# A two-layer decoder on one core: the causal masks of the self-attentions are written into the PSUM banks ahead of the scores, in the scores' own tile shape

## The chip, the cores and the metric

The kernel runs on one core of a Trainium2 chip. The metric is the device time of one execution in microseconds, as the median of several runs. A profile of one further execution gives the trace from which rows are quoted; it has its own time.

## The reference

Eight sequences of 128 tokens with 512 features pass through two post-norm decoder layers. Layer 0 is causal self-attention with 32 heads of 16 features, a cross-attention by autocorrelation against a context, and a mixture of low-rank experts. Layer 1 is causal self-attention with normalised queries and keys and a slope per head (ALiBi), a cross-attention with grouped keys, and a low-rank feed-forward. The change touches the two self-attentions alone:

```python
scores = jnp.einsum('bhqd,bhkd->bhqk', q, k) / math.sqrt(hd)       # layer 0
causal = jnp.tril(jnp.ones((l, l), bool))
scores = jnp.where(causal, scores, -jnp.inf)
att = jax.nn.softmax(scores, axis=-1)
...
scores = jnp.einsum('bqhd,bkhd->bhqk', q, k) * scale               # layer 1
scores = scores + slopes[None, :, None, None] * rel[None, None]
scores = jnp.where(causal[None, None], scores, jnp.float32(-1e+30))
probs = jax.nn.softmax(scores, axis=-1)
```

## The kernel before

A self-attention walks over eight sequences in four steps each (`STEPS = 4`), 32 steps in all, and a step covers eight heads. Queries and keys lie transposed in `qk`, two heads to a strip of 32 partitions (`PAD = 32`): 16 rows of features and beside them rows that carry the slope, the position, block masks (a query block may not see a later key block) and, once known, the row's maximum. So one matmul with 32 rows of contraction gives one head's 128 x 128 scores.

Every step issues two sets of such matmuls from `scores(l, i)`. The first set (L997, step i) writes scores with queries on partitions into the two banks `s_bank`; VectorE takes the maxima of their rows (`maxima`, L2342). The second set (L1002, step i - 5, since `LAG = 5`) writes scores with keys on partitions, with the maxima already subtracted, into the two banks `t_bank`; ScalarE exponentiates them (L1584), and `weigh_values` (L1017) multiplies with the values. Each set has eight matmuls of 32 x 128 weights and 128 columns; four to a bank, and a bank belongs to one strip of 32 rows of the array. The two sets of a step use opposite strips, so that four strips work side by side. Float32 matmuls stand in the trace as two records each.

Only the four diagonal 32 x 32 blocks of each head still need a causal mask. `hide_later` adds it after the scores: per bank four bf16 matmuls of an identity block (32 x 32 weights, `ident16`) with the mask's block repeated for four heads (`causal16`, 32 x 128), each to 32 partitions. The 16 matmuls of a full step fall on the 16 different 32 x 32 tiles of the array. The last of them signals `scores_psum` or `shifted_psum`, for which VectorE and ScalarE wait.

Between two calls of `scores`, TensorE has other work that is written out in a fixed order per step: projections of coming sequences (`mm3`, L840 to L842, three matmuls for a product of split float32r operands), transposes (L949, L890), the output projection, and in a sequence's first step the transpose of its predecessor's maxima (L959). In a sequence's first step the scores also wait for rows that DMAs write into `qk`: in layer 0 and 1 eight `extra` rows (L758 on the SyncE queue, L1565 on ScalarE's for two sequences), signalled by `extra_loaded`, and the maxima (L749), signalled by `max_loaded`. All engines run in the order in which their instructions are written; semaphores tie them together.

Of the kernel before, what the change touches and what calls it, by code (L numbers as in the profile page):

```python
# [13 lines left out]
P = 128  # L14
# [13 lines left out]
RING = 3  # L28
# [19 lines left out]
def shape_constants():  # L48

    t = np.arange(L)  # L50
    ck, sk = np.arange(L // 2 + 1), np.arange(1, L // 2)

    cos_e = lambda n, f: np.cos(2 * np.pi * np.outer(n, f) / L)
    sin_e = lambda n, f: np.sin(2 * np.pi * np.outer(n, f) / L)
    same = np.concatenate([cos_e(t, ck), sin_e(t, sk)], 1)
    swap = np.concatenate([sin_e(t, ck), cos_e(t, sk)], 1)
    weight = np.where((ck == 0) | (ck == L // 2), 1.0, 2.0)

    inv1 = np.concatenate([weight * cos_e(t, ck), 2 * cos_e(t, sk)], 1).T / L
    inv2 = np.concatenate([-weight * sin_e(t, ck), 2 * sin_e(t, sk)], 1).T / L  # L60

    ctx_even = same.copy()
    ctx_even[L - 1, 0] += L

    odd = np.arange(1, 2 * L, 2)[: L // 2]
    ang = lambda n: 2 * np.pi * np.outer(n, odd) / (2 * L)
    lag_odd = np.concatenate([np.cos(ang(t)), np.sin(ang(t))], 1)
    full = np.arange(2 * L)
    co, so = np.cos(ang(full)), np.sin(ang(full))  # L70
    hold = lambda m: np.concatenate([m[: L - 1], m[L - 1:].sum(0, keepdims=True)], 0)
    ctx_odd = np.concatenate([hold(co), hold(so)], 1)
    ctx_odd_swap = np.concatenate([hold(so), hold(co)], 1)

    oute1 = np.concatenate([weight * cos_e(t, ck), 2 * cos_e(t, sk)], 1).T / (2 * L)
    oute2 = np.concatenate([weight * sin_e(t, ck), -2 * sin_e(t, sk)], 1).T / (2 * L)
    outo1 = np.concatenate([2 * np.cos(ang(t)), 2 * np.cos(ang(t))], 1).T / (2 * L)
    outo2 = np.concatenate([2 * np.sin(ang(t)), -2 * np.sin(ang(t))], 1).T / (2 * L)
    tables = [same, ctx_even, swap, ctx_odd, ctx_odd_swap, lag_odd, inv1, inv2, oute1, oute2, outo1, outo2]
    dft = np.stack(tables, 1).astype(np.float32)  # L80

    slopes = (1.0 / np.power(2.0, np.arange(1, H + 1, dtype=np.float32) * (8.0 / H))).astype(np.float32)
    later = np.where(t[:PAD][None, :] > t[:, None] % PAD, -1e30, 0.0)
    sooner = np.where(t[:, None] % PAD > t[:PAD][None, :], -1e30, 0.0)
    masks = np.concatenate([np.eye(P), later, sooner], 1)
    row = np.arange(P) % PAD
    scale, shift = np.zeros((P, 4)), np.zeros((P, 4))
    for which in range(2):
        own, aug = row // HD == which, HD * (1 - which)
        scale[own, which], scale[own, 2 + which] = HD ** -0.5, 1.0  # L90
        shift[row == aug, 2 + which] = 1.0
    extra = np.zeros((2, 2, GROUPS, 4, 2, KT, P))
    head = HT * np.arange(KT)[None, None, :] + 2 * np.arange(GROUPS)[None, :, None] + np.arange(2)[:, None, None]
    extra[1, :, :, 0, 0] = slopes[head][..., None]
    extra[:, :, :, 0, 1] = t - L / 2.0
    for j in range(GROUPS - 1):
        extra[:, :, :, 1 + j, 0] = t // PAD == j
        extra[:, :, :, 1 + j, 1] = np.where(t // PAD > j, -1e30, 0.0)
    small = np.concatenate([scale, shift], 1)
    first_rows = np.repeat(shift[:, :, None], L, 2)  # L100
    for e in range(2):
        for g in range(GROUPS):
            at = g * PAD + HD * (1 - e) + 1
            first_rows[at:at + 4, e:e + 3:2] = extra[0, e, g, :, :, 0]
    return {
        "dft": dft, "masks": masks.astype(np.float32), "small": np.ascontiguousarray(small.astype(np.float32)),
        "extra": extra.astype(np.float32), "first_rows": first_rows.reshape(P, 4 * L).astype(np.float32),
    }
# [7 lines left out]
def decoder(nc, a, out):  # L116
# [9 lines left out]
    with es:  # L126
        place = [ARENA]

        def sb(name, shape, dt=F32):

            at = place[0]
            place[0] += -(-(2 if dt == BF16 else 4) * int(np.prod(shape[1:])) // 32) * 32
            assert place[0] <= ARENA_END, (name, place[0])
            return nc.alloc_sbuf_tensor_at(name, shape, dt, offset=at)
# [55 lines left out]
        (DX, DC, DCS, DO, DOS, DL, I1, I2, E1, E2, O1, O2) = [table[:, i * P:(i + 1) * P] for i in range(12)]  # L190
        br_row = sb("br_row", [P, LH])
        ident = sb("ident", [P, P])
        ident16, causal16 = sb("ident16", [P, P], BF16), sb("causal16", [P, 2, PAD], BF16)
        small = sb("small_sb", [P, 8 + 6 * KT])
        qk_scale, qk_shift = [sb(f"qk_{n}", [P, 2, 2, KT]) for n in ("scale", "shift")]
        row_scale, row_shift = small[:, 0:4], small[:, 4:8]
# [38 lines left out]
        def view(s, at, n, parts=P):  # L235
            return tank[s][0:parts, at:at + n]
# [5 lines left out]
        tok = [view(1, 768 + 512 * i, 512) for i in range(2)]  # L242
        staged = [view(1, 768 + 2 * D * i, 2 * D) for i in range(2)]
        bv_row, bo_row = [view(1, 2816 + D * i, D) for i in range(2)]
        causal = view(1, 3840, 2 * PAD)

        def values_of(s, e):

# [184 lines left out]
        xo_ready = per_slot("xo_ready")  # L433

        TABLES, EARLY, ROWS = 2, 3, 3
        CLOCKED = 17
        W0_TILES = 2 * KT
        X_AT, O_AT = ((0, 1), (1, 1), (1, 0)), (0, 0)
# [162 lines left out]
        def shared(i):  # L602

            return i // STEPS, i % STEPS % 2, i % STEPS // 2
# [12 lines left out]
        def tiles(ap, k=KT):  # L617
            return ap.rearrange("p (k t) -> p k t", k=k)
# [216 lines left out]
        def _(pe):  # L835
# [122 lines left out]
                bank_taken(u)  # L958
                nc.tensor.transpose(m_bank[u % 2][:, 0:P], nm[b % 2], ident[:, :]).then_inc(m_full[u % 2], 1)  # L959

            def hide_later(banks, turned_over):

                for n in range(2):
                    for g in range(GROUPS):
                        rows = (g + 2 * turned_over + n) % GROUPS
                        at, of = slice(g * PAD, (g + 1) * PAD), slice(rows * PAD, (rows + 1) * PAD)
                        ins = mm(tiles(banks[n][:, :])[at, :, at], ident16[of, of],  # L967
                                 causal16[of, turned_over, :].unsqueeze(1).broadcast_to([PAD, KT, PAD]), start=False, stop=True,
                                 skip_group_check=True)
                return ins  # L970

            def scores(l, i):

                j = i - LAG
                if scored(i):
                    b, rows, e = shared(i)
                    if i % STEPS == 0:
                        if (l, b) == (0, 0):
                            pe.wait_ge(first_k, 1)
                            pe.wait_ge(tables_ready, TABLES)  # L980
                        else:
                            pe.wait_ge(qk_rows, batch(l, b, 2, 2))
                            pe.wait_ge(extra_loaded[b % 2], 16 * 2 * GROUPS * (l * B // 2 + b // 2 + b % 2))
                    if l == 0 and i == 2:
                        pe.wait_ge(qk_rows, batch(0, 0, 2, 2))
                    pe.wait_ge(max_ready, step(l, i - 1, 2))
                if scored(j):
                    c, rows_c, f = shared(j)
                    if j % STEPS == 0:
                        pe.wait_ge(max_loaded[c % 2], 32 * (l * B // 2 + c // 2 + 1))  # L990
                    pe.wait_ge(exp_ready, step(l, j - 1, 2))
                for m in range(KT):
                    at = slice(m * P, (m + 1) * P)
                    if scored(i):
                        for n in range(2):
                            g = slice((2 * rows + n) * PAD, (2 * rows + n + 1) * PAD)
                            ins = mm(s_bank[n][:, at], qk[b % RING][g, e, m, :], qk[b % RING][g, 2 + e, m, :], start=m == 0, stop=True,  # L997
                                     skip_group_check=True)
                    if scored(j):
                        for n in range(2):  # L1000
                            g = slice((2 * rows_c + n) * PAD, (2 * rows_c + n + 1) * PAD)
                            ins = mm(t_bank[n][:, at], qk[c % RING][g, 2 + f, m, :], qk[c % RING][g, f, m, :], start=m == 0, stop=True,  # L1002
                                     skip_group_check=True)
                if scored(i):
                    hide_later(s_bank, 0).then_inc(scores_psum, 1)
                if scored(j):
                    hide_later(t_bank, 1).then_inc(shifted_psum, 1)

            def weigh_values(l, b, e):

# [925 lines left out]
        def _(pool):  # L1936
            nc.gpsimd.memset(idle[:, :], 0.0).then_inc(idle_ready, 1)
            nc.gpsimd.memset(half[:, :], -0.5).then_inc(consts_ready, 1)
            for i in range(FREE):
                nc.gpsimd.memset(raw[i][:, 0:1], 0.0).then_inc(w_split, 1)  # L1940
            for i in range(2):
# [283 lines left out]
        def _(dve):  # L2225
# [37 lines left out]

            def tables():

                v.tensor_copy(ident16[:, :], ident[:, :]).then_inc(tables_ready, 1)
                v.tensor_copy(causal16[:, :, :], causal.rearrange("p (a t) -> p a t", a=2)).then_inc(tables_ready, 1)

            def values(l, b):

# [557 lines left out]
```

## Time and profile before

| what | value |
|---|---|
| median of 3 runs | 839.37 us (839.31 to 840.55) |
| the profiled execution | 838.6 us |
| its span, first to last instruction | 836.8 us |
| TensorE matmuls busy | 807.1 us, 96% |
| VectorE / ScalarE / GpSimd busy | 537.8 / 400.9 / 261.3 us |
| mean granted TensorE clock | 0.998 of full speed |

The profiled execution took 0.77 us less than the median, and 1.8 us of it lie outside the span. "Busy" for TensorE counts the time in which at least one matmul is somewhere in the pipeline, so short pauses between dependent groups don't show as idle. To see those, compare the start times of consecutive matmuls in the timeline.

### The profile page before, as it was taken

To read this page: it belongs to the slowest core of one execution; us is meant where nothing else is said; L and a number is where in the kernel's file an instruction comes from. 1 tells how busy PE (TensorE), PEld (TensorE's weight loads), DVE (VectorE), ACT (ScalarE), POOL (GpSimd) and SP (SyncE) were. 2 spreads that over 40 slices of the span, in tenths; PEclk is the share of its full clock that TensorE was granted. 3 is DMA by queue.
4 is the path that set the end of the run, shared out by engine and by line. 5 is a ranking of instruction groups with operands and counts; after the bars stand their busy time and mean duration, and the time that the engine had idled before them with its cause. 6 is when DMAs were issued, how large, how long until landed. Compare 5 with 4: busy or idle time off the path is not lost.

```text
span 836.8 us, 23981 instructions
## 1 busy us (share of the span) xinstructions
PE 807.1 (96%) x10073; PEld 662.7 (79%) x10073; DVE 537.8 (64%) x1379; ACT 400.9 (48%) x989; POOL 261.3 (31%) x311
## 2 busy tenths in 40 slices
PE   8999999999999999999998998999999999999995
PEld 6888887675547787777777787989998899989983
DVE  6675666587886676677776744574466546654666
ACT  4554444558773344455555334463454245424542
POOL 0221422569976632112222368640000100010001
PEclk9999999999999999999999999999999999999999
DMA  9310002222220200000000112330000010000001
GB/s 314 139 53 16 16 22 68 83 52 76 74 63 26 76 20 7 22 22 18 19 18 29 31 40 80 100 102 27 2 3 2 2 52 2 2 1 28 2 2 50
DMA packets 21002, 36.85 MB, mean 44 GB/s; under 512 B 3200, under 2 KB 7424, under 8 KB 20640
## 3 DMA queue, kind: packets, MB, share of 16 engines
q1 hardware_dynamic: 20800, 35.20, 13.6%
q8 instruction: 80, 1.31, 0.7%
q14 instruction: 26, 0.21, 0.1%
q10 hardware_dynamic: 96, 0.13, 0.1%
HBM read 30.86 MB, written 2.10 MB: 39 GB/s over the span
## 4 chain that ended last, share of the span: by engine, by line
PE 81%; DVE 7%; ACT 4%; issue 2%; POOL 2%; DMA 1%; SPq 1%; ACTq 0%; POOLq 0%; DVEq 0%
PE bank L840 16%; PE bank L842 15%; PE bank L841 15%; PE bank L997 6%; PE bank L1277 5%; PE bank L1247 4%; PE bank L1261 3%; PE bank L1017 3%; PE bank L1134 2%; PE bank L1002 2%; DVE tank L2342 1%; PE bank L967 1%; PE bank L1121 1%; PE bank L1298 1%; PE bank L859 1%
## 5 line engine op out<-in xcount | busy, mean ns | idle before, releaser
L840 PE MATMUL bank<-wr,hTl 128*128 128x512 f32 (+3 forms) x392 | 153.3, 391 | 1.3 <-issue 0.8
L842 PE MATMUL bank<-wr,hTh 128*128 128x512 f32 (+3 forms) x392 | 146.9, 375 | 0.0
L841 PE MATMUL bank<-wr,hTh 128*128 128x512 f32 (+3 forms) x392 | 146.5, 374 | 0.0
L1584 ACT ACTIVATE pT<-bank 128x512 f32<-128x512 f32 x128 | 70.0, 604 | 95.1 <-PE bank L967 95.0
L2342 DVE TENSOR_REDUCE tank<-bank 128x4 f32<-128x512 f32 x128 | 82.1, 683 | 42.4 <-PE bank L967 42.4
L840 PEld LDWEIGHTS bank<-wr,hTl 128*128 128x128 f32 (+1 forms) x392 | 73.6, 188 | 17.9 <-issue 5.3
L842 PEld LDWEIGHTS bank<-wr,hTh 128*128 128x128 f32 (+1 forms) x392 | 73.7, 188 | 12.5
L840 PE MATMUL bank<-hTh,wr 128*128 128x256 f32 (+1 forms) x272 | 83.1, 306 | 0.0
L841 PEld LDWEIGHTS bank<-wr,hTh 128*128 128x128 f32 (+1 forms) x392 | 73.8, 188 | 11.2 <-issue 1.0
L841 PE MATMUL bank<-hTl,wr 128*128 128x256 f32 (+1 forms) x272 | 81.0, 298 | 0.0
L842 PE MATMUL bank<-hTh,wr 128*128 128x256 f32 (+1 forms) x272 | 81.0, 298 | 0.0
L997 PE MATMUL bank<-qk 32*128 32x128 f32 x1024 | 74.2, 282 | 7.0 <-DVE tank L2342 2.4
L997 PEld LDWEIGHTS bank<-qk 32*128 32x128 f32 x1024 | 62.3, 186 | 23.0 <-issue 17.2
L1772 ACT ACTIVATE tank<-bank,stats 128x256 f32<-128x256 f32 x128 | 58.6, 484 | 39.6 <-DVE stats L2557 39.6
L1002 PE MATMUL bank<-qk 32*128 32x128 f32 x1024 | 74.2, 283 | 0.3 <-DMA qk<-tank 0.3
L1002 PEld LDWEIGHTS bank<-qk 32*128 32x128 f32 x1024 | 62.0, 186 | 4.0 <-issue 3.0
L2557 DVE TENSOR_REDUCE stats<-bank 128x2 f32<-128x512 f32 x64 | 39.8, 686 | 26.6 <-PE bank L1247 26.6
L2045 POOL TENSOR_TENSOR stats<-stats,half 128x1 f32<-128x1 f32 x7 | 3.8, 547 | 166.8 <-DVE stats L2623 166.8
L1555 ACT ACTIVATE qk<-bank,qk_shift,qk_scale 128x128 f32<-128x128 f32 x128 | 46.6, 476 | 17.4 <-PE bank L949 17.4
L840 PEld LDWEIGHTS bank<-hTh,wr 128*128 128x128 f32 x272 | 51.1, 188 | 4.5 <-issue 0.4
L841 PEld LDWEIGHTS bank<-hTl,wr 128*128 128x128 f32 x272 | 51.1, 188 | 2.1
L842 PEld LDWEIGHTS bank<-hTh,wr 128*128 128x128 f32 x272 | 51.1, 188 | 2.1
(250 smaller groups left out, 1763.8 us busy)
## 6 DMA issues: line engine op xcount, KB each, us to landing
raw<-w_qkv_dram SPq DMA_DIRECT2D x12, 256.0 KB, 2.9
raw<-w_xq_dram SPq DMA_DIRECT2D x16, 192.0 KB, 2.4
raw<-w_xo_dram SPq DMA_DIRECT2D x12, 256.0 KB, 2.8
cin<-xT_dram SPq DMA_DIRECT2D x8, 256.0 KB, 3.9
x_all<-x_dram SPq DMA_DIRECT2D x8, 256.0 KB, 6.6
cin<-ctx_dram SPq DMA_DIRECT2D x8, 256.0 KB, 3.4
cin<-ctxT_dram SPq DMA_DIRECT2D x8, 256.0 KB, 3.3
out_dram<-x_all SPq DMA_DIRECT2D x8, 256.0 KB, 2.1
```

Of the source, the lines that this page charges most:

```text
L840: mm(dst, lhs[1], rhs[0], start=start, stop=False)
L841: mm(dst, lhs[0], rhs[1], start=False, stop=False)
L842: return mm(dst, lhs[0], rhs[0], start=False, stop=stop)
L997: ins = mm(s_bank[n][:, at], qk[b % RING][g, e, m, :], qk[b % RING][g, 2 + e, m, :], start=m == 0, stop=True, skip_group_check=True)
L1002: ins = mm(t_bank[n][:, at], qk[c % RING][g, 2 + f, m, :], qk[c % RING][g, f, m, :], start=m == 0, stop=True, skip_group_check=True)
L1247: ins = mm(scores_bank(n)[:, s * XT:(s + 1) * XT], q[at, c, s, :], xk_parts[c][at, k_lo, s, :], start=q_lo == 1 and c == 0 and s == 0, sto ...
L1277: ins = mm(values_bank(s, g)[rows_of_group(n), c * P:(c + 1) * P], xv[s][:, at:at + PART], xpT[s][:, (2 * n + t) * P:(2 * n + t + 1) * P], ...
L1555: ins = av(qk[b % RING][:, 2 * i + e, m, :], m_bank[u % 2][:, m * P:(m + 1) * P], ACT.Identity, bias=qk_shift[:, i, e, m:m + 1], scale=qk_ ...
L1584: av(pT[e][:, 2 * rows + n, :], t_bank[n][:, :], ACT.Exp).then_inc(exp_ready, 1)
L1772: ins = av(xp[s][:, n * XT:(n + 1) * XT], scores_bank(n)[:, s * XT:(s + 1) * XT], ACT.Exp, bias=st[s][:, NEGMAX.start + n:NEGMAX.start + n ...
L2342: v.tensor_reduce(nm[b % 2][:, at:at + KT], s_bank[n][:, :].rearrange("p (m t) -> p m t", m=KT), AX, ALU.max, negate=True).then_inc(max_re ...
L2557: v.tensor_reduce(stats[:, :, NEGMAX.start + n], scores_bank(n)[:, :].rearrange("p (s t) -> p s t", s=SLOTS), AX, ALU.max, negate=True).th ...
```

## The change

The masks come first. At the start of `scores`, `hide_later` writes them into the banks (`start=True` on the first, so that the bank is opened), and the score matmuls add to them. Their weights are no longer a 32 x 32 identity block but 32 x 128: `band16` holds zeros, an identity block per strip, and zeros again, and a window of 128 columns out of it puts the identity at the columns of block g. So a mask matmul has the tile shape of a score matmul and writes all 128 partitions (zeros outside its block). Each bank's four masks now use the one strip that its scores use. The signals move to the last score matmul of each set. The waits are split: the masks wait for the banks (`max_ready`, `exp_ready`) and once for the tables; the waits for `qk_rows`, `extra_loaded`, `first_k` and `max_loaded` stand behind the masks. Two memsets on GpSimd and a smaller copy on VectorE build the band; the table of masks in DRAM is 32 columns wider.

```diff
-            def hide_later(banks, turned_over):
-
+            def hide_later(banks, turned_over, rows, g, start):
+
+                at = slice(g * PAD, (g + 1) * PAD)
                 for n in range(2):
-                    for g in range(GROUPS):
-                        rows = (g + 2 * turned_over + n) % GROUPS
-                        at, of = slice(g * PAD, (g + 1) * PAD), slice(rows * PAD, (rows + 1) * PAD)
-                        ins = mm(tiles(banks[n][:, :])[at, :, at], ident16[of, of],
-                                 causal16[of, turned_over, :].unsqueeze(1).broadcast_to([PAD, KT, PAD]), start=False, stop=True,
-                                 skip_group_check=True)
+                    of = slice((2 * rows + n) * PAD, (2 * rows + n + 1) * PAD)
+                    ins = mm(tiles(banks[n][:, :])[:, :, at], band16[of, BAND - g * PAD:BAND - g * PAD + P],
+                             causal16[of, turned_over, :].unsqueeze(1).broadcast_to([PAD, KT, PAD]), start=start, stop=False,
+                             skip_group_check=True)
                 return ins
...
+                    if (l, i) == (0, 0):
+                        pe.wait_ge(tables_ready, TABLES)
+                    pe.wait_ge(max_ready, step(l, i - 1, 2))
+                if scored(j):
+                    c, rows_c, f = shared(j)
+                    pe.wait_ge(exp_ready, step(l, j - 1, 2))
+                for g in range(GROUPS):
+                    if scored(i):
+                        hide_later(s_bank, 0, rows, g, g == 0)
+                    if scored(j):
+                        hide_later(t_bank, 1, rows_c, g, g == 0)
+                if scored(i):
                     if i % STEPS == 0:
                         if (l, b) == (0, 0):
                             pe.wait_ge(first_k, 1)
-                            pe.wait_ge(tables_ready, TABLES)
                         else:
                             pe.wait_ge(qk_rows, batch(l, b, 2, 2))
                             pe.wait_ge(extra_loaded[b % 2], 16 * 2 * GROUPS * (l * B // 2 + b // 2 + b % 2))
...
-                if scored(i):
-                    hide_later(s_bank, 0).then_inc(scores_psum, 1)
-                if scored(j):
-                    hide_later(t_bank, 1).then_inc(shifted_psum, 1)
...
             nc.gpsimd.memset(idle[:, :], 0.0).then_inc(idle_ready, 1)
             nc.gpsimd.memset(half[:, :], -0.5).then_inc(consts_ready, 1)
+            nc.gpsimd.memset(band16[:, 0:BAND], 0.0).then_inc(tables_ready, 1)
+            nc.gpsimd.memset(band16[:, BAND + PAD:], 0.0).then_inc(tables_ready, 1)
...
-                v.tensor_copy(ident16[:, :], ident[:, :]).then_inc(tables_ready, 1)
+                v.tensor_copy(band16[:, BAND:BAND + PAD], causal[:, 2 * PAD:]).then_inc(tables_ready, 1)
```

TensorE's instructions at a plain full step of layer 0, before: the end of the two score sets (bank_0 and bank_2 are `s_bank` for L997; bank_3 and another bank_0 are `t_bank`), the masks, and the projection behind them.

```order
L997 MATMUL bank_0<-qk_74 128x128
L997 MATMUL bank_2<-qk_74 128x128
L1002 MATMUL bank_3<-qk_76 128x128
L1002 MATMUL bank_0<-qk_76 128x128
L967 MATMUL bank_0<-causal_56,ident_55 32x4x32 x4
L967 MATMUL bank_2<-causal_56,ident_55 32x4x32 x4
L967 MATMUL bank_3<-causal_56,ident_55 32x4x32 x4
L967 MATMUL bank_0<-causal_56,ident_55 32x4x32 x4
L840 MATMUL bank_1<-wr,hTl 128x512 [waits w0_ready,tok_ready,o_ready]
```

The same step after, from the last projection ahead of it to its first scores (L1005 and L1012 are what L997 and L1002 were).

```order
L843 MATMUL bank_1<-wr 128x512
L967 MATMUL bank_0<-causal_56,band_55 128x4x32 [waits exp_ready,max_ready]
L967 MATMUL bank_2<-causal_56,band_55 128x4x32
L967 MATMUL bank_3<-causal_56,band_55 128x4x32
L967 MATMUL bank_0<-causal_56,band_55 128x4x32 x2
...
L967 MATMUL bank_0<-causal_56,band_55 128x4x32
L1005 MATMUL bank_0<-qk_74 128x128
L1005 MATMUL bank_2<-qk_74 128x128
```

The 16 masks went from behind the scores to ahead of them, in rounds over the four banks (the "..." stands for more rounds), and the projection now follows a score.

The second place is the first step of a sequence in layer 1, on TensorE, before: the transposed maxima and the first scores.

```order
L959 MATMUL bank_1<-ident,tank_66 128x128 [waits tok_raw,max_ready]
L997 MATMUL bank_0<-qk_75 128x128 [waits max_ready,exp_ready,extra_loaded0,qk_rows]
L997 MATMUL bank_2<-qk_75 128x128
L1002 MATMUL bank_3<-qk_76 128x128
L1002 MATMUL bank_0<-qk_76 128x128
```

And after:

```order
L960 MATMUL bank_1<-ident,tank_66 128x128 [waits tok_raw,max_ready]
L967 MATMUL bank_0<-causal_56,band_55 128x4x32 [waits exp_ready,max_ready]
...
L967 MATMUL bank_0<-causal_56,band_55 128x4x32
L1005 MATMUL bank_0<-qk_75 128x128 [waits extra_loaded0,qk_rows]
L1005 MATMUL bank_2<-qk_75 128x128
```

The masks stand between the transpose and the wait for the DMAs' rows; that wait is now the first score's.

## Rows read from the trace of the kernel before

**Rows 1.** The page: busy us, share of span and instructions; granted clock by slice.

```profile
PE 807.1 (96%) x10073; PEld 662.7 (79%) x10073; DVE 537.8 (64%) x1379; ACT 400.9 (48%) x989; POOL 261.3 (31%) x311
PEclk9999999999999999999999999999999999999999
```

**Rows 2.** The page: the chain that ended last, by engine.

```profile
PE 81%; DVE 7%; ACT 4%; issue 2%; POOL 2%; DMA 1%; SPq 1%; ACTq 0%; POOLq 0%; DVEq 0%
```

**Rows 3.** Groups by line and shape, TensorE: busy us, mean ns, idle before.

```profile
L997 PE MATMUL bank<-qk 32*128 32x128 f32 x1024 | 74.2, 282 | 7.0 <-DVE tank L2342 2.4 <-issue 2.0 <-DMA qk<-extra_dram 1.5
L1002 PE MATMUL bank<-qk 32*128 32x128 f32 x1024 | 74.2, 283 | 0.3 <-DMA qk<-tank 0.3
L967 PE MATMUL bank<-causal,ident 32*32 32x128 bf16 x1024 | 19.8, 224 | 0.0
```

**Rows 4.** Timeline of TensorE, one full step: start us, us, instruction.

```profile
109.04 0.28 PE L841 MATMUL bank<-wr 128*128 128x256 f32 x1
109.16 0.28 PE L842 MATMUL bank<-wr 128*128 128x256 f32 x1
109.37 0.38 PE L997 MATMUL bank<-qk 32*128 32x128 f32 x2
109.58 0.28 PE L997 MATMUL bank<-qk 32*128 32x128 f32 x2
109.70 0.28 PE L997 MATMUL bank<-qk 32*128 32x128 f32 x2
...
110.25 0.28 PE L997 MATMUL bank<-qk 32*128 32x128 f32 x2
110.27 0.28 PE L1002 MATMUL bank<-qk 32*128 32x128 f32 x2
110.47 0.28 PE L967 MATMUL bank<-causal,ident 32*32 32x128 bf16 x16
110.68 0.43 PE L1017 MATMUL bank<-pT,tank 128*32 128x128 f32 x8
```

**Rows 5.** Timeline of TensorE, a step with one score set.

```profile
323.57 1.16 PE L997 MATMUL bank<-qk 32*128 32x128 f32 x16
324.66 0.25 PE L967 MATMUL bank<-causal,ident 32*32 32x128 bf16 x8
324.84 0.33 PE L890 MATMUL bank<-ident,x_all 128*128 128x128 f32 x1
```

**Rows 6.** Weight loads by line: ns min/median/max, shapes.

```profile
L911 PEld LDWEIGHTS bank<-idle x17: 98/98/152, 1.0 to 5.5; 128*128 128x128 bf16 x17
L967 PEld LDWEIGHTS bank<-causal,ident x1024: 87/87/88, 22.0 to 485.8; 32*32 32x32 bf16 x171
L949 PEld LDWEIGHTS bank<-ident,tank x64: 137/140/146, 305.4 to 447.0; 128*128 128x128 f32 x64
L997 PEld LDWEIGHTS bank<-qk x1024: 181/187/188, 20.9 to 468.7; 32*128 32x128 f32 x171
```

**Rows 7.** Timeline of weight loads: ten bf16 loads, one per 512 columns.

```profile
3.52 2.10 PEld L911 LDWEIGHTS bank<-idle 128*128 128x128 bf16 x10 [0.28 <-issue]
```

**Rows 8.** Waits of TensorE: us in total, times, longest.

```profile
PE bank L997 <- DVE tank L2342: 2.4, 6, 0.5
PE bank L997 <- issue: 2.0, 5, 0.6
PE bank L997 <- DMA qk<-extra_dram: 1.5, 2, 0.8
PE bank L1002 <- DMA qk<-tank: 0.3, 1, 0.3
```

**Rows 9.** Timeline of TensorE and of SyncE's queue, first step of a sequence.

```profile
390.55 5.67 SPq L758 DMA_DIRECT2D qk<-extra_dram  x8
396.97 0.27 PE L959 MATMUL bank<-ident,tank 128*128 128x128 f32 x1
397.85 0.38 PE L997 MATMUL bank<-qk 32*128 32x128 f32 x2 [0.61 <-issue]
```

**Rows 10.** Timeline, layer 1: the first scores of the third sequence.

```profile
376.70 0.38 PE L997 MATMUL bank<-qk 32*128 32x128 f32 x2 [0.42 <-issue]
376.88 0.31 PE L997 MATMUL bank<-qk 32*128 32x128 f32 x2
```

More of the change, by code:

```diff
@@ L84, in shape_constants @@
     sooner = np.where(t[:, None] % PAD > t[:PAD][None, :], -1e30, 0.0)
-    masks = np.concatenate([np.eye(P), later, sooner], 1)
+    masks = np.concatenate([np.eye(P), later, sooner, np.tile(np.eye(PAD), (GROUPS, 1))], 1)
     row = np.arange(P) % PAD
@@ L192, in decoder @@
         ident = sb("ident", [P, P])
-        ident16, causal16 = sb("ident16", [P, P], BF16), sb("causal16", [P, 2, PAD], BF16)
+        BAND = P - PAD
+        band16, causal16 = sb("band16", [P, BAND + P], BF16), sb("causal16", [P, 2, PAD], BF16)
         small = sb("small_sb", [P, 8 + 6 * KT])
@@ L244, in decoder @@
         bv_row, bo_row = [view(1, 2816 + D * i, D) for i in range(2)]
-        causal = view(1, 3840, 2 * PAD)
+        causal = view(1, 3840, 3 * PAD)
         def values_of(s, e):
@@ L433, in decoder @@
         xo_ready = per_slot("xo_ready")
-        TABLES, EARLY, ROWS = 2, 3, 3
+        TABLES, EARLY, ROWS = 4, 3, 3
         CLOCKED = 17
@@ L985, in scores @@
                         pe.wait_ge(qk_rows, batch(0, 0, 2, 2))
-                    pe.wait_ge(max_ready, step(l, i - 1, 2))
-                if scored(j):
[L988 to L991, printed above, removed]
+                if scored(j) and j % STEPS == 0:
+                    pe.wait_ge(max_loaded[c % 2], 32 * (l * B // 2 + c // 2 + 1))
                 for m in range(KT):
                     at = slice(m * P, (m + 1) * P)
+                    last = m == KT - 1
                     if scored(i):
@@ L996, in scores @@
                             g = slice((2 * rows + n) * PAD, (2 * rows + n + 1) * PAD)
-                            ins = mm(s_bank[n][:, at], qk[b % RING][g, e, m, :], qk[b % RING][g, 2 + e, m, :], start=m == 0, stop=True,
+                            ins = mm(s_bank[n][:, at], qk[b % RING][g, e, m, :], qk[b % RING][g, 2 + e, m, :], start=False, stop=True,
                                      skip_group_check=True)
+                        if last:
+                            ins.then_inc(scores_psum, 1)
                     if scored(j):
@@ L1001, in scores @@
                             g = slice((2 * rows_c + n) * PAD, (2 * rows_c + n + 1) * PAD)
-                            ins = mm(t_bank[n][:, at], qk[c % RING][g, 2 + f, m, :], qk[c % RING][g, f, m, :], start=m == 0, stop=True,
+                            ins = mm(t_bank[n][:, at], qk[c % RING][g, 2 + f, m, :], qk[c % RING][g, f, m, :], start=False, stop=True,
                                      skip_group_check=True)
-                if scored(i):
-                    hide_later(s_bank, 0).then_inc(scores_psum, 1)
-                if scored(j):
-                    hide_later(t_bank, 1).then_inc(shifted_psum, 1)
+                        if last:
+                            ins.then_inc(shifted_psum, 1)
             def weigh_values(l, b, e):
@@ L2264, in tables @@
             def tables():
-                v.tensor_copy(ident16[:, :], ident[:, :]).then_inc(tables_ready, 1)
-                v.tensor_copy(causal16[:, :, :], causal.rearrange("p (a t) -> p a t", a=2)).then_inc(tables_ready, 1)
+                v.tensor_copy(band16[:, BAND:BAND + PAD], causal[:, 2 * PAD:]).then_inc(tables_ready, 1)
+                v.tensor_copy(causal16[:, :, :], causal[:, 0:2 * PAD].rearrange("p (a t) -> p a t", a=2)).then_inc(tables_ready, 1)
             def values(l, b):
```

## The prediction

> **What bounds the kernel now.** I read the page first. TensorE is busy for 807.1 of 836.8 us, no other engine for more than 64%, and its granted clock is at the full 2.4 GHz in every slice [rows 1]. The chain that ended last runs on TensorE for 81% of the span [rows 2]. So a change pays by what it takes out of TensorE's stream, or out of the few waits in it. The groups by line then look harmless: the 1024 mask matmuls have 19.8 us busy and no idle before them [rows 3]. That number misleads, since a matmul lasts 224 ns in the pipeline while up to 16 of them overlap; what a group costs stands in the start times.
>
> The timeline of a full step shows them. Inside a stream of projections the starts are 0.12 us apart (109.04 to 109.16). The first scores come 0.21 us after the last projection, the second pair 0.21 us after the first, and from there a pair every 0.112 us (109.58 to 110.25 in six gaps) [rows 4]. So whenever the tile shape changes, some 0.09 us pass before the first matmul and some 0.10 us more before the second, whose weights cannot have been loaded behind anything. The masks start 0.20 us behind the last score, and the next shape 0.21 us behind the masks [rows 4]. Without masks the next shape would start about 0.20 us behind the last score, as the masks do. **The masks of a full step cost 0.21 us today**, not because of their columns but because of two changes of shape where one would do. In a step with one set, the last score starts at 323.57 + 1.16 - 0.28 = 324.45, the masks at 324.66 and the next at 324.84: 0.18 us [rows 5].
>
> There are 1024 mask matmuls [rows 3] in two layers, 512 in each. With 32 steps and a lag of 5, each layer has 27 steps with both sets (16 masks) and 10 with one (8 masks); 27 x 16 + 10 x 8 = 512. So 54 full steps and 20 half steps.
>
> **The masks in the new form.** The four banks' strips work side by side, but the four masks of one bank now follow each other on one strip. So there are four rounds instead of one.
> - A round: 128 bf16 columns. Ten bf16 matmuls of 512 columns came (2.10 - 0.10) / 9 = 0.222 us apart [rows 7]; a quarter is 0.056 us. A float32 record of 128 columns needs 0.112 us [rows 4], two passes, which gives the same 0.056. Three gaps between rounds: 0.17 us.
> - The first score's weights: its load can start once the last mask round has moved into the array. Score pairs follow at 0.112 us with the same load [rows 4]; I take 0.11 us from the last round to the first score.
> - The second score pair then follows after 0.11 instead of 0.21 us, since the array is already in this shape and loads run ahead: 0.10 us back.
> - The cost is 0.17 + 0.11 - 0.10 = 0.18 us (0.175 unrounded), against 0.21 in a full step and 0.18 in a half step. Gain 0.035 x 54 = **1.9 us** in full steps, none in half steps.
>
> What decides this is how long a mask's weights take to load, which no row has in this very form (32 x 128, bf16). The nearest is 128 x 128 bf16 at 98 ns, against 87 ns for the masks now, 140 ns for a float32 transpose's weights and 187 ns for a score's [rows 6]. All hold a fixed part; by the differences, the new masks load in about 11 ns more than the old ones and 89 ns less than a score. If a score's load just keeps up with 0.112 us a round, the new one fills some 0.02 us and hides behind 0.056 us of columns. Bounds: as slow as a transpose's, 0.04 us more than I take (140 against 98), it costs only the first gap, +0.05 us x 74 = +3.7 us; as slow as a score's, below in the rivals. On the other side, if the first score's load were hidden too, 0.055 us x 74 = 4.1 us more would be gained.
>
> A rule of the Trainium skill speaks against the change: "TensorE: Matmul & The Clock Gate", section on LDWEIGHTS, puts a load at columns / 1.2 ns, whatever the rows. It makes the new weights four times as long as the old, 107 against 27 ns. The same page's section on Fast Weight Load excepts loads of 128 columns that are not float32. The 98 ns row, only 11 above the 32-column one, sides with the exception; by the plain rule the sum would be that of the third rival.
>
> **The waits.** TensorE waits before scores for rows that a DMA writes: five times 2.0 us in all (named "issue"), twice 1.5 us for `extra`, once 0.3 us for the maxima [rows 8]. The five are of one kind: SyncE issues eight `extra` DMAs from 390.55 to 396.22, TensorE finishes its transpose at 396.97 and can't start the scores before 397.85 [rows 9]. These eight waits (3.8 us) now stand behind the masks. The banks are free by then, so the masks run in what was idle. At 376.70 the first score comes after a wait and the second pair 0.18 us later [rows 10], in the new form 0.11 later. So such a step saves the 0.21 us of masks and 0.07: 0.28 us, of which 0.035 is counted above. The shortest idles are about as long as the block. Seven full steps x 0.245 and 0.17 for the half one: **1.9 us**.
>
> Part is lost again. The DMA chain starts from TensorE's own transposes two to three steps earlier; what the two steps between save (2 x 0.035) only lengthens the wait: 8 x 0.07 = 0.5 us back.
>
> The waits for VectorE's maxima (2.4 us in six [rows 8]) stay ahead of the whole block. Their loop is scores, signal, VectorE, next scores. Counted from the block's start, the first set was signalled when the first eight masks ended, 1.10 + 0.02 + 0.22 = 1.34 us [rows 4]; now by the last score, 0.28 + 7 x 0.112 + 0.28 = 1.34. Nothing changes for VectorE, nor for ScalarE's exponentials.
>
> Edits that I cost at nothing: VectorE's copy of 128 x 32 in place of 128 x 128, two short memsets on GpSimd, 16 KB more of tables at the start. They save or cost at most about 0.1 us each, and all come before the first scores at 20.9 us.
>
> **Sum:** -1.9 - 1.9 + 0.5 = -3.3 us. The profiled execution of 838.6 us would become 835.3; on the median of 839.37 that is **836.1 us**. This case alone I give 833 to 838: the lower end goes most of the way to the hidden score load (4.1 us more, 832.0), the upper one halfway to rival 1.
>
> **The rivals.**
> 1. The rounds are dearer and eat the rest: the load takes as long as a transpose's, +3.7 us on -3.3 us, so 839.8. No change. For it: the loads of four strips start within nanoseconds of each other. Against: scores load 32 times per step in this way and keep 0.112 us.
> 2. The rounds are as forecast, but the waits don't shrink, since the DMAs' landing sets what follows and TensorE is waited for nowhere else: only the 1.9 us remain, 837.5. Against it: behind each of these waits the trace shows TensorE busy with projections for whole steps.
> 3. Slower: the masks' weights load at a score's pace. From this row on it decides: 187 ns instead of 98 [rows 6]. Then mask rounds behave as scores do, 0.21 + 3 x 0.11 = 0.54 us up to the first score, less 0.10, so 0.44 against 0.21: +0.23 x 54 + 0.26 x 20 = +17.6 us, of which the eight waits hide up to 3.3. That gives 853.7. The break-even is where a round reaches about 0.07 us. A sibling: the step from bf16 masks to float32 scores stops the array as a change of shape does. Then 0.10 is added and the 0.10 is not given back, +0.2 x 74 = +14.8 - 3.3, about 851. The trace has no such pair back to back inside one shape, so it can't be excluded.
> 4. The change does not do what it says: the first score's second load still waits as it does now (0.21 between pairs), though the shape is the same. +0.10 x 74 - 3.3 = +4.1, 843.5.
>
> **How the numbers follow.** Forecast 0.50; rival 1 0.15; rival 2 0.15; rivals 3 and its sibling 0.13; rival 4 0.07. A measurement of this kernel tells 0.2%, 1.7 us, from no change. The forecast is faster nearly throughout (0.48), rival 2 lies at that edge (0.10 faster, 0.05 same), rival 1 splits (0.05 faster, 0.08 same, 0.02 slower): faster 0.63, same 0.15, slower 0.22. The range from 833.0 to 842.0 leaves out rivals 3 and 4, together 0.20, and takes in all else.
>
> **What the profile after would show.** In a full step: masks 0.21 us behind the last projection, first scores 0.28 us behind the first masks, pairs at 0.11 us from the first gap on, and the next shape 0.20 us behind the last score. Weight loads of the masks near 98 ns. The waits named "issue" and `extra` in sum down from 3.8 to about 2 us. If the first scores come 0.5 us behind the masks, rival 3 is right; if the second gap among scores is still 0.2, rival 4. The waits for VectorE's maxima should keep their 2.4 us; if they grow, the signal comes later than I worked out.

## The result, and the profile after

The change made the kernel slower: 841.51 us (median of 19 runs, 840.34 to 844.62) against 839.37 us (19 runs), a ratio of 1.0024 with a 95% interval of 1.0016 to 1.0032. The forecast was 836.1 us and faster; the measured time lies within its range of 833 to 842, near the upper end, and on the wrong side of the time before.

The page of the changed kernel, beside [rows 1]: busy us by engine and the granted clock by slice. L841 to L843 are what L840 to L842 were, L1005 and L1012 what L997 and L1002 were.

```profile
span 839.7 us, 23980 instructions
PE 813.8 (97%) x10073; PEld 671.6 (80%) x10073; DVE 535.8 (64%) x1379; ACT 400.8 (48%) x989; POOL 260.3 (31%) x313
PEclk9999999999999999999999999999999999999998
```

TensorE has the same 10073 matmuls, and they are busy 6.7 us longer. The clock is the same. I looked first where I had expected the gain, at the full step of [rows 4], in the timeline of TensorE:

```profile
109.27 0.28 PE L843 MATMUL bank<-wr 128*128 128x256 f32 x1
109.48 0.40 PE L967 MATMUL bank<-causal,band 32*128 32x128 bf16 x16
109.71 0.33 PE L1005 MATMUL bank<-qk 32*128 32x128 f32 x2
...
109.87 0.27 PE L1005 MATMUL bank<-qk 32*128 32x128 f32 x2
...
110.55 0.27 PE L1012 MATMUL bank<-qk 32*128 32x128 f32 x2
110.75 1.08 PE L1025 MATMUL bank<-pT,tank 128*32 128x128 f32 x32
```

The masks start 0.21 us behind the projection, their 16 starts spread over 0.40 - 0.21 = 0.19 us, and the block from masks to next shape takes 110.75 - 109.48 = 1.27 us where it took 1.31. The weight loads of the masks are as short as was argued (min/median/max ns):

```profile
L967 PEld LDWEIGHTS bank<-causal,band x1024: 90/93/94, 21.0 to 483.8; 32*128 32x128 bf16 x171
```

The self-attentions really end earlier. Their last product with the values (first and last start, of before and of after):

```profile
L1017 PE MATMUL bank<-pT,tank x1024: 272/273/298, 48.2 to 489.3; 128*32 128x128 f32 x171
```

```profile
L1025 PE MATMUL bank<-pT,tank x1024: 272/273/298, 48.2 to 488.2; 128*32 128x128 f32 x171
```

So the changed kernel leads by 1.1 us at 488 us, and loses 4 us in the 350 us behind that, in which the change has no instruction. The key matmuls of the second cross-attention mark that stretch, before and after:

```profile
L1247 PE MATMUL bank<-xk,wr x720: 270/274/388, 525.5 to 804.8; 32*128 32x256 f32 x180
```

```profile
L1255 PE MATMUL bank<-xk,wr x720: 269/277/387, 524.3 to 807.6; 32*128 32x256 f32 x180
```

From the first to the last it took 279.3 us and takes 283.3 us. In a stream of 256-column projections within it the loss can be read off one start after the other. Before:

```profile
607.63 0.28 PE L841 MATMUL bank<-hTl,wr 128*128 128x256 f32 x1
607.75 0.28 PE L842 MATMUL bank<-hTh,wr 128*128 128x256 f32 x1
607.86 0.28 PE L840 MATMUL bank<-hTh,wr 128*128 128x256 f32 x1
...
608.99 0.28 PE L841 MATMUL bank<-hTl,wr 128*128 128x256 f32 x1
```

After:

```profile
607.56 0.28 PE L842 MATMUL bank<-hTl,wr 128*128 128x256 f32 x1
607.68 0.28 PE L843 MATMUL bank<-hTh,wr 128*128 128x256 f32 x1
607.80 0.28 PE L841 MATMUL bank<-hTh,wr 128*128 128x256 f32 x1
...
608.88 0.28 PE L841 MATMUL bank<-hTh,wr 128*128 128x256 f32 x1
```

Twelve gaps took 608.99 - 607.63 = 1.36 us, 113 ns each; eleven gaps now take 608.88 - 607.56 = 1.32 us, 120 ns each. Three lines of 180 such matmuls stand between 510 and 806 us; 540 times 7 ns are 3.8 of the 4 us. Another 124 gaps of this kind lie before 500 us and grew from 114 to 119 ns, 0.6 us. The instructions, their operands and their order are the same. What differs is where the operands lie: `band16` takes 448 bytes per partition where `ident16` took 256, and every tensor that is allocated behind it, the activations `hTh` and `hTl` included, moved by 192 bytes. The weights `wr` are allocated ahead of it and stayed.

### The profile page after: what moved, and what is told of

It reads as the page before. It is cut to its first block, busy times and chain, and to the rows that moved or that the text cites. A ratio compares the mean times of both kernels' runs of the same rounds, so it can differ in the third digit from the quotient of the medians.

```text
span 839.7 us, 23980 instructions
## 1 busy us (share of the span) xinstructions
PE 813.8 (97%) x10073; PEld 671.6 (80%) x10073; DVE 535.8 (64%) x1379; ACT 400.8 (48%) x989; POOL 260.3 (31%) x313
## 3 DMA queue, kind: packets, MB, share of 16 engines
q8 instruction: 80, 1.31, 0.7%
## 4 chain that ended last, share of the span: by engine, by line
PE 79%; DVE 7%; ACT 5%; SPq 2%; issue 2%; POOL 2%; DMA 2%; ACTq 0%; POOLq 0%; DVEq 0%
PE bank L841 16%; PE bank L843 14%; PE bank L842 14%; PE bank L1005 5%; PE bank L1285 5%; PE bank L1255 4%; PE bank L1269 3%; PE bank L1142 2%; PE bank L1025 2%; PE bank L967 2%; SPq L759 2%; DVE tank L2352 1%; PE bank L1012 1%; PE bank L1129 1%; ACT qk L1563 1%
## 5 line engine op out<-in xcount | busy, mean ns | idle before, releaser
L841 PE MATMUL bank<-wr,hTl 128*128 128x512 f32 (+3 forms) x392 | 153.8, 392 | 1.1 <-DVE hTl L2538 0.6
L843 PE MATMUL bank<-wr,hTh 128*128 128x512 f32 (+3 forms) x392 | 147.3, 376 | 0.0
L842 PE MATMUL bank<-wr,hTh 128*128 128x512 f32 (+3 forms) x392 | 147.0, 375 | 0.0
L841 PEld LDWEIGHTS bank<-wr,hTl 128*128 128x128 f32 (+1 forms) x392 | 73.7, 188 | 18.9 <-issue 4.9
L841 PE MATMUL bank<-hTh,wr 128*128 128x256 f32 (+1 forms) x272 | 84.3, 310 | 0.0
L843 PEld LDWEIGHTS bank<-wr,hTh 128*128 128x128 f32 (+1 forms) x392 | 73.7, 188 | 12.9
L842 PEld LDWEIGHTS bank<-wr,hTh 128*128 128x128 f32 (+1 forms) x392 | 73.9, 188 | 11.6 <-issue 1.0
L843 PE MATMUL bank<-hTh,wr 128*128 128x256 f32 (+1 forms) x272 | 82.1, 302 | 0.0
L842 PE MATMUL bank<-hTl,wr 128*128 128x256 f32 (+1 forms) x272 | 82.0, 301 | 0.0
L1005 PE MATMUL bank<-qk 32*128 32x128 f32 x1024 | 71.3, 277 | 1.7 <-DMA qk<-extra_dram 1.6
L1012 PE MATMUL bank<-qk 32*128 32x128 f32 x1024 | 71.5, 277 | 0.0
L1005 PEld LDWEIGHTS bank<-qk 32*128 32x128 f32 x1024 | 62.3, 187 | 2.7 <-issue 2.6
L1012 PEld LDWEIGHTS bank<-qk 32*128 32x128 f32 x1024 | 62.3, 187 | 0.0
L841 PEld LDWEIGHTS bank<-hTh,wr 128*128 128x128 f32 x272 | 51.2, 188 | 5.2 <-issue 0.4
L842 PEld LDWEIGHTS bank<-hTl,wr 128*128 128x128 f32 x272 | 51.3, 188 | 2.1
L843 PEld LDWEIGHTS bank<-hTh,wr 128*128 128x128 f32 x272 | 51.2, 188 | 2.2
```

Of the source, the lines that this page charges most:

```text
L841: mm(dst, lhs[1], rhs[0], start=start, stop=False)
L842: mm(dst, lhs[0], rhs[1], start=False, stop=False)
L843: return mm(dst, lhs[0], rhs[0], start=False, stop=stop)
```

## The experiments

**Is it the place?** Two kernels part the change from the shift. The first keeps the change and gives every other tensor its old address.

```diff
-        band16, causal16 = sb("band16", [P, BAND + P], BF16), sb("causal16", [P, 2, PAD], BF16)
+        sb("hole", [P, P], BF16)
+        causal16 = sb("causal16", [P, 2, PAD], BF16)
...
         xk_last = sb("xk_last", [P, 2, SLOTS, XT], F32R)
+        band16 = sb("band16", [P, BAND + P], BF16)
```

> The change as made, but the band lies behind all other tensors in SBUF and a hole of the old identity's 256 bytes stays in its place, so every other tensor has its address of before. Theory P (place): the change moved every tensor allocated behind the band, the activations hTh and hTl, the tanks and x_all among them, by 192 bytes, and that slows the 256-column projections of the second half from 113 to 120 ns each. Then this run has them back at 113 ns, the stretch from 495 us on is as long as before, and the time is 837.3 us, 2 us under the kernel before. Rival I (instruction stream: something in the program's length, order or state slows later matmuls): spacing 120 ns and 841.5 us, as the change measured.

The second is the kernel before with the shift alone.

```diff
-        ident16, causal16 = sb("ident16", [P, P], BF16), sb("causal16", [P, 2, PAD], BF16)
+        ident16 = sb("ident16", [P, P], BF16)
+        sb("hole", [P, P - PAD], BF16)
+        causal16 = sb("causal16", [P, 2, PAD], BF16)
```

> The kernel before with nothing changed but 192 unused bytes behind the bf16 identity, so that the later tensors lie where the changed kernel has them. Theory P: the spacing of 256-column projections goes from 113 to 120 ns and the time to about 842.5 us (before + 3.5). Rival I: no change, 839.4 us.

Measured: with the band last 837.22 us, ratio to before 0.9979 (0.9971 to 0.9988); before with the shift 844.22 us, ratio 1.0058 (1.0046 to 1.007). The stream of projections in the first of them, with its own line numbers:

```profile
605.74 0.28 PE L844 MATMUL bank<-hTl,wr 128*128 128x256 f32 x1
605.86 0.28 PE L845 MATMUL bank<-hTh,wr 128*128 128x256 f32 x1
...
607.11 0.28 PE L844 MATMUL bank<-hTl,wr 128*128 128x256 f32 x1
```

Twelve gaps in 1.37 us, 114 ns. Its key matmuls run from 523.9 to 803.2 us, 279.3 us as before:

```profile
L1257 PE MATMUL bank<-xk,wr x720: 270/274/387, 523.9 to 803.2; 32*128 32x256 f32 x180
```

The place costs 841.51 - 837.22 = 4.3 us with the change, and 5.0 us without it, where 3.5 were expected. Rival I is out: the same instructions run at the old pace as soon as the tensors are back. And the masks in front are, by themselves, worth 2.0 us (837.22 against 839.22 in the same set of runs).

**What of the 2.0 us is waits, and what is order?** Both kernels start from the one with the band last.

```diff
-                for g in range(GROUPS):                      # ahead of the waits
-                    if scored(i):
-                        hide_later(s_bank, 0, rows, g, g == 0)
-                    if scored(j):
-                        hide_later(t_bank, 1, rows_c, g, g == 0)
...
                 if scored(j) and j % STEPS == 0:
                     pe.wait_ge(max_loaded[c % 2], 32 * (l * B // 2 + c // 2 + 1))
+                for g in range(GROUPS):                      # the same lines behind them
...
```

> As e1, but all waits of the scores (qk_rows, extra_loaded, first_k, max_loaded) stand ahead of the masks, as they stood ahead of the scores. If the masks hide in these eight waits, this run loses what that gave: about 1.5 us more than e1, 838.8 us, with the masks waiting 3.5 us or more in sum for DMAs. If the waits merely move (my second rival), it equals e1 within 0.3 us.

The second of them puts the masks behind the scores. The lines for `t_bank` change in the same way, `hide_later` closes the bank's group (`stop`), and the masks ahead of the scores and the signals on the last score are gone.

```diff
-                            ins = mm(s_bank[n][:, at], ..., start=False, stop=True,
+                            ins = mm(s_bank[n][:, at], ..., start=m == 0, stop=True,
...
+                for g in range(GROUPS):
+                    if scored(i):
+                        ins = hide_later(s_bank, 0, rows, g, False)
+                        if g == GROUPS - 1:
+                            ins.then_inc(scores_psum, 1)
+                    if scored(j):
+                        ins = hide_later(t_bank, 1, rows_c, g, False)
+                        if g == GROUPS - 1:
+                            ins.then_inc(shifted_psum, 1)
```

> As e1, but the band-shaped masks follow the scores, with the signals on the last mask of each set: the new shape alone, without the new order. By my accounting the masks in front save the 0.10 us of the second gap and hide in waits; behind the scores the block is 0.21 + 6 x 0.112 + 0.015 for the scores, some 0.08 to the first mask, 3 x 0.056 and 0.20 to the next shape: 1.34 us against 1.27 in front and 1.31 before. Time about 841.5 us (e1 + 0.07 x 74 - and no hiding). If a bf16 load behind a score is free, 840 us.

With all waits ahead of the masks: 838.41 us, 1.2 us over the one with the band last; ratio to before 0.9997 (0.9985 to 1.0008). So the hiding is worth 1.2 us, where 1.5 were expected (0.4 to 2.0 when the single times of the two kernels are resampled), and what is left of the gain, 0.8 us, is not clear of zero by itself. TensorE's waits (total us, times, longest) name it, now with the mask's line in the place that the score has in [rows 8]:

```profile
PE bank L969 <- DMA qk<-extra_dram: 3.9, 7, 0.9
```

Compare one of the seven places, the third sequence in layer 1 ([rows 10] has it before). First with the waits in front, then with the band last and the waits behind the masks:

```profile
375.55 0.27 PE L962 MATMUL bank<-ident,tank 128*128 128x128 f32 x1
...
376.30 0.40 PE L969 MATMUL bank<-causal,band 32*128 32x128 bf16 x16 [0.48 <-DMA qk<-extra_dram]
376.52 0.34 PE L1007 MATMUL bank<-qk 32*128 32x128 f32 x2
```

```profile
375.25 0.27 PE L962 MATMUL bank<-ident,tank 128*128 128x128 f32 x1
375.45 0.40 PE L969 MATMUL bank<-causal,band 32*128 32x128 bf16 x16
375.91 0.38 PE L1007 MATMUL bank<-qk 32*128 32x128 f32 x2
```

In the second the masks follow the transpose after the usual 0.20 us, and the first score comes 0.66 us behind the transpose in place of 0.97. Over the whole kernel with the band last, the waits of this block for ScalarE and for these rows are:

```profile
PE bank L969 <- ACT pT L1594: 1.6, 3, 1.1
PE bank L1007 <- DMA qk<-extra_dram: 1.0, 3, 0.4
```

The waits for DMAs are down from 3.8 us in eight places to 1.0 us in three. But in two of the eight places the masks now wait for ScalarE to release their banks (0.27 us at 454.47 and 0.17 us at 471.92 in its timeline; the third of these waits, 1.1 us long, stood before too). The prediction took the banks to be free by then; in these two places they were not.

With the band-shaped masks behind the scores: 840.79 us, ratio 1.0015 (1.0005 to 1.0025), 3.6 us over the one with them in front. Expected were 4.3. The block in its timeline:

```profile
110.33 0.38 PE L1001 MATMUL bank<-qk 32*128 32x128 f32 x2
110.54 0.28 PE L1001 MATMUL bank<-qk 32*128 32x128 f32 x2
...
111.22 0.28 PE L1006 MATMUL bank<-qk 32*128 32x128 f32 x2
111.32 0.40 PE L969 MATMUL bank<-causal,band 32*128 32x128 bf16 x16
111.65 0.32 PE L1026 MATMUL bank<-pT,tank 128*32 128x128 f32 x4
```

It takes 1.32 us. No shape changes between score and mask any more (0.10 instead of 0.20 us), but the second score gap is back at 0.21 and four rounds take longer than 16 masks side by side. The new shape alone is 1.6 us slower than the kernel before; it pays only in front, where the second gap is 0.16 instead of 0.21 us and the masks run during waits. Of the 3.6 us the waits are 1.2, so the order alone is worth 2.4 us.

**Which place, and relative to what?** Four kernels without the change, that is, the kernel before with tensors moved: all of them by 192 bytes, or the activations alone (a hole directly ahead of `hTh`) by 192, 64 and 128.

```diff
-ARENA, ARENA_END = 16512, 229344
+ARENA, ARENA_END = 16512 + 192, 229344
```

```diff
+        sb("hole", [P, 96], BF16)      # 192 bytes; [P, 32] and [P, 64] for 64 and 128
         at_hT = place[0]
```

> The kernel before with 192 unused bytes directly ahead of hTh, so that of the large tensors only hTh, hTl and xk_last move. If these alone carry the loss (their projections are the ones that slowed), 120 ns spacing and most of the +5.0 us of the earlier shift: 843 to 844 us. If x_all, the contexts and the tanks carry it, 839 to 840 us.

> The same with 64 bytes. hTh lies at 320 modulo 512 before, 0 after the change, 384 here. If the loss grows with the shift in steps, this lies between: spacing 115 to 118 ns, 840 to 842 us. If only certain positions collide (the one with offset 0), 113 ns and 839.3 us.

> The same with 128 bytes, offset 448 modulo 512. By the first view above 117 to 120 ns and 841 to 843 us; by the second 113 ns and 839.3 us.

And four with the change and the band last, whose unused 256 bytes are shortened by 64, 128, 192 and 256, so that all tensors behind it come closer to the weights.

```diff
-        sb("hole", [P, P], BF16)
+        sb("hole", [P, 96], BF16)      # 64 bytes closer; 64, 32 and none for 128, 192 and 256
```

> The change with the band last (837.2 us), and the hole left by the old identity shortened from 256 to 192 bytes: every tensor behind it, activations included, lies 64 bytes closer to the weights. Distance of hTh from the start of the weights modulo 512: 128 (192 before, 256, 320 and 384 in the three shifted runs). Theory R says that the distance counts, not which size it has: if the old distance was by chance the best one, this loses some 2 to 4 us (839 to 841); if the loss is a valley with its floor on this side, it is 836 to 838 us.

> The same, hole of 128 bytes, distance 64 modulo 512. If positions within 256 bytes of each other's line collide, 839 to 842 us; a shift that leaves columns of 256 at 113 ns gives 837 us.

> The same, hole of 64 bytes, distance 0 modulo 512. If the pattern repeats after 256 bytes, this is the 64-byte shift once more: 2 us over the band-last kernel, 839.2; otherwise open, 837 to 842.

> The same without any hole, distance 448 modulo 512. If the pattern repeats after 256 bytes, this equals the band-last kernel: 837.2 us and 113 ns. If it repeats only after 512, there is no reason for that and 839 to 842 us are likelier.

The times, ordered by how far `hTh` moved against the weights, modulo 256 bytes. "Own base" is the kernel before (839.2 to 839.5 in its three sets of runs) or the band-last one (837.22).

| moved by, mod 256 | kernel | us | over its own base | ratio to before (95%) |
|---|---|---|---|---|
| 0 | all tensors +192 | 839.04 | -0.5 | 0.9995 (0.9986 to 1.0005) |
| 0 | change, band last, 256 closer | 837.05 | -0.2 | 0.9974 (0.9963 to 0.9985) |
| 64 | before, +64 | 841.42 | +1.9 | 1.0031 (1.0018 to 1.0043) |
| 64 | change, band last, 192 closer | 839.71 | +2.5 | 1.0004 (0.9995 to 1.0014) |
| 128 | before, +128 | 843.24 | +3.7 | 1.005 (1.0035 to 1.0065) |
| 128 | change, band last, 128 closer | 840.61 | +3.4 | 1.0013 (1.0003 to 1.0023) |
| 192 | before, +192 | 843.54 | +4.0 | 1.0053 (1.0036 to 1.007) |
| 192 | change, band last, 64 closer | 841.77 | +4.6 | 1.0027 (1.0016 to 1.0037) |

Theory R holds: moving everything costs nothing, and moving the activations against the weights does. The two lines of each pair, one moved apart and one moved together, agree within 0.6 us, so over these moves, all multiples of 64 bytes, it is the position modulo 256 bytes that counts. Three runs left their expected ranges: 64 bytes on, the spacing was 120 and not 115 to 118 ns; 128 bytes on, the time was 843.24 and not at most 843; and 64 bytes closer, it was 841.77 and not at most 841.

The groups by line and shape between 510 and 806 us show the same in the mean duration of a 256-column projection (the second number behind the bar, ns), one kernel a fence. Before, and before with the activations 64 and 128 bytes on:

```profile
L842 PE MATMUL bank<-hTh,wr 128*128 128x256 f32 x180 | 49.8, 277 | 0.0
```

```profile
L843 PE MATMUL bank<-hTh,wr 128*128 128x256 f32 x180 | 50.9, 283 | 0.0
```

```profile
L843 PE MATMUL bank<-hTh,wr 128*128 128x256 f32 x180 | 50.2, 279 | 0.0
```

The one with the band last and the tensors 192 bytes closer, which is the partner of the 64 bytes above:

```profile
L845 PE MATMUL bank<-hTh,wr 128*128 128x256 f32 x180 | 50.9, 283 | 0.0
```

The changed kernel, and the one with the band last and no hole:

```profile
L843 PE MATMUL bank<-hTh,wr 128*128 128x256 f32 x180 | 50.8, 282 | 0.0
```

```profile
L844 PE MATMUL bank<-hTh,wr 128*128 128x256 f32 x180 | 49.9, 277 | 0.0
```

By the starts in this stretch, the median gap of such matmuls is 113 to 114 ns at 0, 120 at 64, 118 at 128 and 119 to 120 at 192. A control stands in the same traces: the 182 gaps of 256-column projections whose two operands both lie in `wr` (the `bank<-wr` lines of [rows 4]) have a median of 119 ns in each of these kernels.

Matmuls of 512 columns behave otherwise. Most of them have the roles reversed, with `wr` as columns and the activations as weights (`bank<-wr,hTh`): 229 to 230 ns at 0, 227 at 64, 233 at 128 and 232 at 192. Those with the activations as columns have 235 ns at 0 and 227 at 64 too. They gain where the 256-column ones are at their slowest, which fits that 64 bytes cost less than 128.

## Why the prediction was wrong

- **The step that failed** stands under the edits that were costed at nothing: "VectorE's copy of 128 x 32 in place of 128 x 128, two short memsets on GpSimd, 16 KB more of tables at the start. They save or cost at most about 0.1 us each". The list leaves out that the wider table moves every tensor behind it in SBUF, so the sum holds this term at nothing. It costs 4.3 us (the changed kernel against the one with the band last), more than all that the change saves. It is shown in both directions, by giving the tensors back their places and by moving them without the change. None of my rivals had it: rivals 3 and 4, which end slower, look for the loss inside the mask block, and most of it lay in projections 40 us and more behind the last mask (483.9 us).
- **Full steps.** Forecast 0.035 us each, 1.9 us in all. The block went from 1.31 to 1.28 us; summed over the 54 full blocks of the kernel with the waits in front (worked out from the starts in the traces) it is 70.95 - 69.41 = 1.5 us. Of its parts, the first score came 0.23 us behind the masks and not 0.28, and the second gap was 0.16 and not 0.11; the two errors cancel, which is luck. The mask rounds took 0.058 us each, against 0.056.
- **Half steps.** Forecast no change; 1.27 us both before and after.
- **Waits.** Forecast 1.9 us hidden; the two kernels that differ in it alone measure 1.2. Two of the eight places lost part of it to ScalarE, as shown above. The waits for DMAs were to fall from 3.8 to about 2 us; they fell to 1.6 in the changed kernel and 1.0 with the band last. My second rival, that the waits would merely move, is out, if narrowly: it asked for less than 0.3 us.
- **Given back.** Forecast 0.5 us, since shorter blocks only lengthen the waits. It came: all waits ahead of the score blocks are 7.3 us in the timeline of before and 7.8 in that of the kernel with the waits in front.
- **Weight loads.** Forecast near the 98 ns row; measured 93 ns, half of a score's load of the same 32 x 128. So the third rival, with a score's 187 ns, is out, and its sibling too, since the first score starts 0.04 us behind the last mask, sooner than the 0.11 us that were taken. The plain rule of the Trainium skill ("TensorE: Matmul & The Clock Gate", section on LDWEIGHTS), which counts columns alone, is out for this load. The exception in the page's section on Fast Weight Load agrees with these 93 ns. The first rival (a transpose's 140 ns) is out too; its price of 3.7 us was worked out with 0.05 us where 140 - 98 ns gives 3.1. The fourth is out in the main: the second gap shrank from 0.21 to 0.16, half of the 0.10 us that was to come back.
- **VectorE's maxima.** Forecast unchanged; TensorE waits 2.3 us in six for them ahead of the masks, against 2.4 [rows 8].
- **The sum.** The terms measured give -1.5 + 0.5 - 1.2 = -2.2 us in the attentions, where -3.3 were forecast; the kernel with the band last measures -2.0 against before, and its last product with the values starts at 487.4 us, 1.9 us ahead of before. So what the prediction said of the mask block itself was right in its mechanism, and the gain came out a third smaller. With the 4.3 us of the place it comes out slower, 841.51 against 839.37 us.
## What to carry to other kernels

An edit that changes the size of one tensor moves all that are allocated behind it. In a kernel bound by TensorE, compare the spacing of matmuls that the change didn't touch before you judge the change itself, and put new or grown tensors last, or keep the old footprint. Here that turned a loss of 0.24% into a gain of 0.21 to 0.26%. A change of tile shape that is followed by a wait is a good place for small matmuls of the coming shape: they pay for the change of shape and hide in the wait, as far as the banks that they write are free by then.

## What the runs showed of the hardware

- Streams of 128 x 128 float32r matmuls with 256 columns run at 113 to 120 ns each, by the position of their columns against their weights modulo 256 bytes, at the same granted clock (0.99 to 1.00). Over the whole kernel that is up to 4.6 us of 837, from moves of 64 to 192 bytes. No single position is best for all: 512 columns are fastest (227 ns) where 256 columns are slowest. Where neither operand moved, the pace stayed at 119 ns in every one of these kernels.
- Inside one tile shape, bf16 masks followed by float32 scores need no pause of their own: the first score started 0.04 us behind the last mask's start (109.71 against 109.48 + 0.19). The pair after it came 0.16 us later, 0.05 us more than the pairs behind that take.
- A change of tile shape costs about 0.09 us on top of what the last matmul's columns take. From the last start of one shape to the first of the next, the traces of before and after have 0.20 us behind 128 float32 columns, 0.20 to 0.21 behind 256 columns, 0.27 behind 384 and 0.32 to 0.33 behind 512; behind the 128 bf16 columns of the old masks it is 0.15. Where the new shape starts with float32 scores, the second pair then comes after 0.21 us instead of 0.11.
